# The last four passes of a pipelined transformer kernel, written out call by call on all five engines

## What is computed

```
x = x + tanh(g_xattn[0]) * L0_xattn(layernorm(x), ctx, ctx)   # q, k, v with relu; relu(q k') v, no softmax
x = x + tanh(g_ffn[0])   * L0_ffn(layernorm(x))               # 512 -> 1024 -> 1024 -> 256, weights +1 or -1
x = x + tanh(g_xattn[1]) * L1_xattn(layernorm(x), ctx)        # best key of each token, then softmax over 77 keys, 16 heads
x = x + tanh(g_ffn[1])   * L1_ffn(layernorm(x))               # shared expert + top 8 of 64 experts, 128 rows each

# L1_ffn:
probs = softmax(x @ gate_w); w, idx = top_k(probs, 8)
pos = running count of the tokens that chose an expert        # over all tokens, in order
buf[e, slot] = x[tok]; act = silu(gate) * up; out_e = act @ expert_down_w
y = sum over the 8 chosen of out_e[e, slot] * w, where pos < 128
```

## Time and profile before

| | us |
|---|---|
| median of 3 runs | 1708.06 |
| lowest and highest | 1705.67, 1710.39 |
| the profiled execution | 1710.62 |
| its span in the trace | 1708.9 |
| busy in the span: PE, DVE, ACT, POOL | 1533.9, 1312.4, 1018.1, 1006.8 |

### The profile page before, as it was taken

One profiled execution on the slowest core, in us unless ns is written; L12 is line 12 of the kernel. 1 busy time (PEld: TensorE's weight loads), 2 busy tenths in 40 slices (PEclk: granted clock), 3 DMA queues, 4 the chain that ended last, 5 costly groups with the idle time before them and its releaser, 6 DMA issues.

```text
span 1708.9 us, 50224 instructions
## 1 busy us (share of the span) xinstructions
PE 1533.9 (90%) x15780; PEld 1308.4 (77%) x15780; DVE 1312.4 (77%) x4611; ACT 1018.1 (60%) x2789; POOL 1006.8 (59%) x1517
## 2 busy tenths in 40 slices
PE   2879999999999999999999999999999986478885
PEld 1768888888888888888888888888888865367774
DVE  5468888888888888888888888888888865456564
ACT  2456666666666666666666666666666653334443
POOL 3114566666666666666666666666666644365554
PEclk8989999999999999999999999999999997799998
DMA  7624444444433333433333333333333334558886
GB/s 224 190 55 101 101 102 100 93 98 99 87 74 79 84 82 83 92 77 77 80 84 80 84 77 77 77 80 81 80 81 77 91 67 111 126 139 207 201 196 129
DMA packets 382151, 176.21 MB, mean 103 GB/s; under 512 B 310175, under 2 KB 371561, under 8 KB 382104
## 3 DMA queue, kind: packets, MB, share of 16 engines
q1 hardware_dynamic: 348312, 156.45, 38.8%
q0 software_dynamic: 33792, 19.17, 6.6%
HBM read 51.63 MB, written 111.84 MB: 96 GB/s over the span
## 4 chain that ended last, share of the span: by engine, by line
PE 62%; DMA 14%; issue 8%; DVE 7%; ACT 4%; POOL 3%; SPq 1%; POOLq 0%; DVEq 0%; ACTq 0%
PE bank L1306 24%; PE bank L1200 9%; DMA out<-h_h,aid 9%; PE ps_yo L1200 7%; PE ps_yo L1322 3%; PE bank L1288 3%; DMA pt<-p_hl 3%; PE ps_m L1200 2%; PE ps_pt L1200 2%; PE ps_lg L1370 2%; PE ps_pt L1272 2%; ACT p L977 2%; POOL table L722 2%; PE ps_pt L1265 1%; PE ps_tr L1200 1%
## 5 line engine op out<-in xcount | busy, mean ns | idle before, releaser
L722 POOL DMA_INDIRECT table<-xs,slot x496 | 511.7, 1032 | 189.5 <-issue 158.3
L769 POOL TENSOR_TENSOR rs<-nt,minushalf 128x2 f32<-128x2 f32 x128 | 95.6, 747 | 311.4 <-DVE nt L1756 310.9
L977 ACT ACTIVATE p<-ps_lg,rmax 128x77 f32<-128x77 f32 x1024 | 248.6, 335 | 50.9 <-DVE rmax L1868 49.4
L1306 PE MATMUL bank<-h_h,held 128*128 128x256 f16 x2048 | 266.2, 273 | 1.4 <-DVE h_l L1798 1.1
L1306 PE MATMUL bank<-h_l,held 128*128 128x256 f16 x2048 | 265.7, 273 | 0.0
L1306 PEld LDWEIGHTS bank<-h_l,held 128*128 128x128 f16 x2048 | 200.6, 98 | 23.4
L1306 PEld LDWEIGHTS bank<-h_h,held 128*128 128x128 f16 x2048 | 195.4, 98 | 27.6 <-issue 1.6
L1798 DVE SCALAR_TENSOR_TENSOR h_l<-bank,h_h 128x512 f16<-128x512 f32 x256 | 172.7, 684 | 33.3 <-ACT h_h L954 23.8
L949 ACT ACTIVATE h_h<-bank 128x512 f16<-128x512 f32 x128 | 76.4, 597 | 156.1 <-PE bank L1288 156.1
L1200 PE MATMUL bank<-xt,gu_h 128*128 128x256 f16 x1024 | 157.1, 277 | 3.1 <-DVE ac L1964 2.9
L1288 PE MATMUL bank<-xt,held 128*128 128x256 f16 x1024 | 134.1, 282 | 22.8 <-DMA xt<-rows_hl 13.4
(11 more groups left out here) (271 smaller groups left out, 3884.8 us busy)
## 6 DMA issues: line engine op xcount, KB each, us to landing
ew<-in_e_wts SPq DMA_DIRECT2D x48, 384.0 KB, 3.9
table<-xg SPq DMA_DIRECT2D x8, 1284.0 KB, 14.8
xg<-table SPq DMA_DIRECT2D x64, 160.5 KB, 3.4
xs<-xr SPq DMA_DIRECT2D x31, 320.0 KB, 2.8
x<-in_x SPq DMA_DIRECT2D x32, 256.0 KB, 2.8
out<-x SPq DMA_DIRECT2D x32, 256.0 KB
table<-xs,slot POOLq DMA_INDIRECT x496
held<-in_e_wts SPq DMA_DIRECT2D x16, 384.0 KB, 5.0
```

Of the source, the lines that this page charges most:

```text
L722: return g.indirect_dma_start(out=table, out_offset=bass.IndirectOffsetOnAxis(ap=slots[:, t, k:k + 1], axis=0), in_=rows[:, t, :], in_offs ...
L769: g.tensor_tensor(rs[i][:, :], nt[i][:, 0, :], minushalf[:, :], ALU.pow).then_inc(ln_root[i], 1)
L977: ins = a.activation(p32[r % 2][:, h * S2:(h + 1) * S2], ps_lg[:, g_, h % HB * S2:(h % HB + 1) * S2], ACT.Exp, bias=rmax[r % 2][:, h:h + 1])
L1306: ins = mm(two(bank[j % 2])[:, m % 2, :], wb1[:, k, m * P:(m + 1) * P], hp[:, k, :], start=(i == 0 and k == 0), stop=(i == 1 and k == FK - 1))
```

## The change

The calls of `body` behind the loop are replaced, on every engine, by the calls that they would make, each with its block as a constant, in another order. The functions themselves, the loop, the prologue and the expert phase are the same. No wait is added or removed; where a wait stands in the engine's order changes. SP's list is short and stands here in full; of the others a few lines.

```diff
@@ sync
             body(NB - 2)
             for i in range(4):
                 load_held(i)
-            body(NB - 1)
+            turn_p(2, NB - 3)
+            turn_p(3, NB - 3)
+            turn(1, NB - 1)
+            pass_rows(NB - 4)
+            stack(NB - 2)
+            turn(3, NB - 3)
+            turn_p(0, NB - 2)
+            turn_p(1, NB - 2)
+            store_x4(NB - 4)
+            turn_p(2, NB - 2)
+            turn_p(3, NB - 2)
+            pass_rows(NB - 3)
+            stack(NB - 1)
+            turn(3, NB - 2)
+            turn_p(0, NB - 1)
+            store_x4(NB - 3)
+            turn_p(1, NB - 1)
+            turn_p(2, NB - 1)
+            pass_rows(NB - 2)
+            turn_p(3, NB - 1)
             for i in range(4, 8):
                 load_held(i)
             for e in range(XD - 1):
                 load_weights(e, e)
-            body(NB)
+            turn(3, NB - 1)
             sp.wait_ge(l2_rdy, NB)
             for i in range(8, 12):
                 load_held(i)
-            body(NB + 1)
+            pass_rows(NB - 1)
+            store_x4(NB - 2)
             for i in range(12, 16):
                 load_held(i)
-            body(NB + 2)
+            store_x4(NB - 1)
@@ gpsimd
-            body(NB - 1)
-            body(NB)
-            body(NB + 1)
-            body(NB + 2)
+            keep_x2(NB - 3)
+            ln_coef(1, NB - 1)
+            ln_coef(2, NB - 2)
+            keep_x1(NB - 1)
+            scatter('a', NB - 4)
...
@@ tensor
-            body(NB - 1)
-            body(NB)
-            body(NB + 1)
+            d_gu(0, NB - 4)
+            c_lg(2, NB - 3)
...
             d_gu(0, NB - 1)
             d_gu(1, NB - 1)
+            d_cp(NB - 1)
             d_gu(2, NB - 1)
-            d_cp(NB - 1)
...
@@ vector, the last block's part D
             d_max(NB - 1)
+            d_choose(NB - 1)
             d_gu(0, NB - 1)
-            d_choose(NB - 1)
...
```

More of the change, by code:

```diff
@@ new lines, in _ @@
+            c_qp(NB - 2)
+            ln_norm(3, NB - 3, x3, xr)
+            high(3, NB - 3, xr[:, :, 0:D])
+            c_stack(NB - 2)
+            b_l1(0, NB - 1)
+            b_l1(1, NB - 1)
+            c_vb(NB - 2)
+            c_exp(0, NB - 2)
+            d_gu(0, NB - 3)
+            c_exp(1, NB - 2)
+            d_ac(0, NB - 3)
+            d_gu(1, NB - 3)
+            c_phi(0, NB - 2)
+            d_gu(2, NB - 3)
+            c_exp(2, NB - 2)
+            d_ac(1, NB - 3)
+            c_exp(3, NB - 2)
@@ new lines, in _ @@
+            c_qp(NB - 1)
+            ln_norm(3, NB - 2, x3, xr)
+            high(3, NB - 2, xr[:, :, 0:D])
+            c_stack(NB - 1)
+            c_vb(NB - 1)
+            c_exp(0, NB - 1)
+            c_exp(1, NB - 1)
+            c_phi(0, NB - 1)
+            c_exp(2, NB - 1)
+            d_gu(0, NB - 2)
+            c_exp(3, NB - 1)
+            d_gu(1, NB - 2)
+            d_ac(0, NB - 2)
+            c_phi(1, NB - 1)
+            c_exp(4, NB - 1)
+            d_gu(2, NB - 2)
+            c_exp(5, NB - 1)
@@ new lines, in _ @@
+            c_phi(2, NB - 1)
+            d_ac(1, NB - 2)
+            d_route(NB - 2)
+            c_exp(6, NB - 1)
+            c_exp(7, NB - 1)
+            d_ac(2, NB - 2)
+            c_phi(3, NB - 1)
+            d_gu(3, NB - 2)
+            d_ac(3, NB - 2)
+            high(4, NB - 1, att[:, :, :])
+            ln_norm(3, NB - 1, x3, xr)
+            high(3, NB - 1, xr[:, :, 0:D])
+            d_route(NB - 1)
+            d_gu(0, NB - 1)
+            d_gu(1, NB - 1)
+            d_ac(0, NB - 1)
@@ L1155, in rows_copy @@
+            d_ac(1, NB - 1)
+            d_gu(2, NB - 1)
+            d_gu(3, NB - 1)
+            d_ac(2, NB - 1)
+            d_ac(3, NB - 1)
             def rows_copy(e, u):
@@ new lines, in _ @@
+            c_lg(7, NB - 3)
+            b_l1(5, NB - 2)
+            b_l1(6, NB - 2)
+            d_dn(0, NB - 4)
+            d_dn(1, NB - 4)
+            c_av(1, NB - 3)
+            b_l1(7, NB - 2)
+            d_cp(NB - 4)
+            c_av(2, NB - 3)
+            b_l2(0, NB - 2)
+            b_l2(1, NB - 2)
+            c_av(3, NB - 3)
+            b_l0(0, NB - 1)
+            across(4, NB - 3)
+            b_l0(1, NB - 1)
+            c_wc(NB - 3)
+            across(2, NB - 2)
+            b_l0(2, NB - 1)
@@ new lines, in _ @@
+            c_lg(4, NB - 2)
+            b_l1(4, NB - 1)
+            c_lg(5, NB - 2)
+            b_l1(5, NB - 1)
+            b_l1(6, NB - 1)
+            c_lg(6, NB - 2)
+            c_av(0, NB - 2)
+            d_cp(NB - 3)
+            c_lg(7, NB - 2)
+            d_dn(0, NB - 3)
+            d_dn(1, NB - 3)
+            c_av(1, NB - 2)
+            b_l1(7, NB - 1)
+            c_av(2, NB - 2)
+            b_l2(0, NB - 1)
+            b_l2(1, NB - 1)
+            c_av(3, NB - 2)
+            across(4, NB - 2)
@@ L1598, in _ @@
+            c_av(0, NB - 1)
+            c_lg(7, NB - 1)
+            c_av(1, NB - 1)
+            d_cp(NB - 2)
+            c_av(2, NB - 1)
+            d_dn(0, NB - 2)
+            c_av(3, NB - 1)
+            across(4, NB - 1)
+            d_dn(1, NB - 2)
+            c_wc(NB - 1)
             d_route(NB - 1)
@@ new lines, in _ @@
+            c_max(7, NB - 3)
+            c_plo(2, NB - 3)
+            d_ac(2, NB - 4)
+            d_ac(3, NB - 4)
+            c_norm(0, NB - 3)
+            c_plo(3, NB - 3)
+            ln_shift(1, NB - 1)
+            b_l1(2, NB - 2)
+            c_norm(1, NB - 3)
+            d_x4(NB - 4)
+            low(1, NB - 1, xn[1][:, :, :])
+            d_pos(NB - 4)
+            b_l1(3, NB - 2)
+            c_norm(2, NB - 3)
+            d_slots(NB - 4)
+            b_x2(NB - 2)
+            c_norm(3, NB - 3)
@@ new lines, in _ @@
+            d_gu(3, NB - 3)
+            c_plo(1, NB - 2)
+            c_max(5, NB - 2)
+            d_choose(NB - 3)
+            d_ac(2, NB - 3)
+            d_ac(3, NB - 3)
+            c_plo(2, NB - 2)
+            c_max(6, NB - 2)
+            d_pos(NB - 3)
+            b_l1(2, NB - 1)
+            c_norm(0, NB - 2)
+            c_max(7, NB - 2)
+            d_x4(NB - 3)
+            c_norm(1, NB - 2)
+            c_plo(3, NB - 2)
+            b_l1(3, NB - 1)
+            d_slots(NB - 3)
+            c_norm(2, NB - 2)
@@ new lines, in _ @@
+            b_x2(NB - 1)
+            ln_sums(2, NB - 1, x2, x2_ok)
+            c_norm(3, NB - 2)
+            ln_moments(2, NB - 1)
+            ln_shift(2, NB - 1)
+            low(4, NB - 2, att[:, :, :])
+            low(2, NB - 1, xn[2][:, :, :])
+            c_x3(NB - 2)
+            ln_sums(3, NB - 2, x3, x3_ok)
+            ln_moments(3, NB - 2)
+            c_qp(NB - 1)
+            ln_shift(3, NB - 2)
+            c_argmax(NB - 1)
+            c_counts(NB - 1)
+            low(3, NB - 2, xr[:, :, 0:D])
@@ L2148, in _ @@
+            d_choose(NB - 2)
+            c_norm(0, NB - 1)
+            d_ac(1, NB - 2)
+            c_plo(3, NB - 1)
+            d_pos(NB - 2)
+            c_norm(1, NB - 1)
+            d_gu(3, NB - 2)
+            d_ac(2, NB - 2)
+            c_norm(2, NB - 1)
+            d_ac(3, NB - 2)
+            d_slots(NB - 2)
+            c_norm(3, NB - 1)
+            low(4, NB - 1, att[:, :, :])
+            d_x4(NB - 2)
+            c_x3(NB - 1)
+            ln_sums(3, NB - 1, x3, x3_ok)
             ln_moments(3, NB - 1)
```

243 lines of the change are left out of this document (233 added, 10 removed).

## The result

| | before | changed kernel |
|---|---|---|
| median, us (4 runs each, side by side) | 1707.11 | 1687.58 |
| lowest and highest | 1705.67, 1710.39 | 1683.97, 1689.96 |
| the profiled execution (the one before is not among its four runs) | 1710.62 | 1689.96 |
| its span | 1708.9 | 1688.2 |

The ratio is 0.9881, with a 95% interval of 0.9854 to 0.9908: 19.5 us less by the medians, where the forecast had 17.8 less.

The account below looks back on a forecast made before the run. The tail was taken as a chain of block 31 alone, held by what stands in its way. Seven stage terms sum to -17.8 us: 1692.8 for the profiled execution, 1690.3 against the 1708.06 median; range 1683 to 1701.

Parts of the forecast that it names:

- Pass 31: Pass from 1348.6 on, 48.0 us: PE's 4.51 us wait for `att` goes, clock nearly 1.00; 43.0 us, minus 5.0.
- End of the first feed-forward: Block 31's stage after pass 31, 24.8 us: short PE waits shrink; 21.4 to 26, taken as 23.5, minus 1.3.
- To the first logits: Block 31's next stage, 22.2 us: DVE's 4.34 us wait goes, with most of PE's 5.46; minus 5.4.
- Softmax: Block 31, first logits to last `c_av`, 28.4 us: transpose saves 3.2, logits order 1.88 and 1.8; 21.5, minus 6.9.
- To part D's input: Block 31, last `c_av` to part D input's landing, 15.9 us: DVE order and seven loads cost 0.5 each; plus 1.0.
- My 13.3 us: Price of seven weight loads and the copy behind them, ahead of part D's transpose, wanted 15.9 us later: 2.6 in hand.
- Part D: Block 31, part D up to the first expert, 19.2 us: earlier choice, slots and `x4`; minus 1.2.
- Expert phase: Last window, 201.8 us: part of the last four weight loads still under way at the first `xg`; plus 1.0.
- the weights land in front: Rival: weight loads ahead of block 31's part D transpose make part D start late; 1698.3 us, chance 0.13.
- The waits only change places: Rival: stages two and four don't gain, as one more engine waits for PE's order; 1698.5 us, chance 0.12.
- The clock comes back: Rival: fuller stages three to five are granted 2.4 GHz on PE; another -3.8 us, 1686.5, chance 0.12.
- POOL's queue: Rival: weight loads slow POOL's 29 scatters, so first expert's rows come late; over 5.1 us slower; 0.04 with other losses.

Follow-up runs that it names:

- the second profile: The changed kernel called again with nothing edited, beside its variants: median 1685.06 us, ratio 0.9861 to the kernel before, span 1682.1 us.
- the kernel with eleven loads: The changed kernel with four more weight loads, eleven instead of seven, ahead of the transpose of block 31's part D input: ratio 0.9875 to the kernel before.

## Why the prediction was right, and where not

The time was right: 1690.3 forecast, 1687.6 measured, and the range held it. By its steps (the first profile and the second):

- **Pass 31**, 43.0 forecast: 46.1 and 42.7. The mechanism is shown from both sides: with the `pow` in front of the scatters 42.3 to 46.4 us, with POOL's old list 48.3 to 56.1. I had priced the transposes behind four loads at up to 1 us on PE; it is 2.03 in one execution (1.1 in the second), and the clock takes 1.7 more (16 matmuls at a pitch of 0.21 us instead of 0.11).
- **End of the first feed-forward**, 23.5 forecast: 22.2 and 22.0. Right in sign, the gain was sized too small: 1.3 against 2.6. PE is busy for 21.31 us of it, so it came to within 1 us of my lower end of 21.4. I had read the edits here as small repairs. The experiments show more: with POOL's list alone, the computing engines' alone, or these two, this stage is 29.7 to 32.3 us, through `d_slots(29)` and through `pt`, in one case by way of SP's own wait for scatters. I had seen neither of these two couplings.
- **To the first logits**, 16.8 forecast: 17.8 and 16.6. The wait of 4.34 us on DVE fell to 0.85. Shown by undoing it: with POOL's old list the stage takes 23.3 us, and DVE waits again, 5.96 us; with POOL's and SP's new lists alone it takes 17.9.

```profile
1435.16 0.16 DVE L1971 TENSOR_TENSOR nb<-nt,rs 128x2 f32<-128x2 f32 x1 [5.96 <-POOL rs L789]
```

  The computing engines' lists alone have 16.7 us here with POOL's old list. That is no counterexample: PE's wait of 6.72 us comes first, so POOL is through its scatters in time (its `pow` waits 2.18 us for DVE), and this stage and the one before it last 46.5 us together, against 47.0 before and 40.1 in the changed kernel.
- **Softmax**, 21.5 forecast: 20.0 and 20.2. The transpose's part was 3.2 us; from the end of the low half to the last `c_av` it is 3.9 us now and was 6.8:

```profile
1448.11 0.83 DVE L2141 TENSOR_TENSOR p_hl<-p,p_hl 128x640 f16<-128x640 f32 x1 [0.17 <-ACT p_hl L1062]
```

```profile
1447.24 0.69 SPq L485 DMA_DIRECT2D xs<-xr  x1
1449.00 1.37 SPq L474 DMA_TRANSPOSE pt<-p_hl  x1
1450.42 2.11 SPq L575 DMA_DIRECT2D held<-in_e_wts  x4
1452.57 1.73 SPq L572 DMA_DIRECT2D ew<-in_e_wts  x3
...
1463.61 1.25 SPq L463 DMA_TRANSPOSE xt<-rows_hl  x1
...
1472.57 2.21 SPq L575 DMA_DIRECT2D held<-in_e_wts  x4
```

  The other two parts had 3.7 us, and took 5.5: from the first logits to the end of the last low half it is 16.1 us (1448.94 - 1432.85) and was 21.6. ACT's wait of 1.88 us before its last exponentials is gone. So the estimate of 1.8 us from PE's idle time was the weak term: by difference it wants about 3.6, and no run takes it apart. That `pass_rows(30)` costs nothing held: it went out at 1447.24, 14.4 us after the first logits (15 forecast), and the transpose found SP free at 1449.00.
- **To part D's input**, plus 1.0 forecast: -1.5 and -0.1. This is the step that failed. The seven loads were issued at 1450.42 and the transpose at 1463.61, when its rows were ready; it landed 3.64 us later, as one without loads in front. The DMA row of 1448 to 1500, 1.3 us to a number, shows the queue empty by 1461:

```profile
GB/s 231 136 219 227 333 310 331 392 388 117 0 0 8 191 254 367 324 271 61 296 228 265 237 390 208 0 0 0 163 277 29 120 42 85 24 120 232 171 310 196
```

  So the seven took under 11 us with block 30's scatters beside them. My 13.3 us were read from the first load's issue to the first scatter behind the copy. That holds the copy too, which is no small transfer as I called it (320 KB, a load has 384), and two transposes had been queued ahead of the loads and two more behind the copy. A time from issue to landing holds everything that was in the queue.
- **Part D**, 18.0 forecast: 19.8 and 17.3. It can't be judged to the 1.2 us of the forecast, since the clock (0.76 and 0.89) moves it by more. That the scatters would wait for their slots and not for POOL was right:

```profile
1477.93 0.97 POOL L742 DMA_INDIRECT table<-xs_z,slot_z  x1 [3.07 <-DVE slot_z L2219]
```

- **Expert phase**, 202.8 forecast: 201.1 and 200.1. The plus 1.0 for leftover weights isn't there, for the same reason: the DMA row above is at zero again from 1480.5 to 1484.4, so the last four loads, issued at 1472.57, were through before the first `xg` went out at 1484.65.

So four of the seven stages came out 1.1 to 2.7 us shorter than forecast, and in the first profile pass 31 and part D gave 4.9 us of that back. Its stages sum to -18.9 us against the earlier trace rows, those of the second profile to -25.6: the forecast of -17.8 lies near the medians' -19.5, and 6.0 us from the -23.8 of the second set. Its terms were too cautious, so part of the match with the first set is luck.

Of the rivals, *the weights land in front* is excluded by the row above and by the profile of the kernel with eleven loads. *The waits only change places* did not come for the whole, but it is just what single lists do. *The clock comes back* is not seen: PE's clock in stages three to five is 0.69, 0.68, 0.85 and 0.84, 0.75, 0.61, against 0.71, 0.74, 0.61 before. The softmax, with PE busy for 64 to 68% of it instead of 55%, is still in good part at 1.2 GHz. The Trainium skill (TensorE: Matmul & The Clock Gate, What's actually happening) says that activity releases the clock. By that rule this case was to come; here PE's busy share rose and the granted clock of the softmax went from 0.74 to 0.68 and 0.75. *POOL's queue* is out, by POOL's waits between 1347 and 1487, to set beside the earlier trace rows:

```profile
POOL rs L789 <- DVE nt L2024: 29.6, 5, 16.4
POOL table L742 <- issue: 21.0, 62, 3.1
```

Its scatters' issue waits are as before, 0.34 us in the mean (20.5 us in 59 waits before), and it has idle time to give.

## What to carry to other kernels

Where each engine takes its instructions in a fixed order, an order is one decision over all engines: a list tried on one engine alone can come out slower, as SP's did here by 5.3 us, though the whole is 20 us faster. So look for a short operation with a waiting engine behind it (here a `pow` of 0.7 us) that stands behind work that itself waits, move it in front, and ask of every reordered engine which tile, transpose, copy or scatter another engine still delivers in the old order. Price a queue of DMAs by when the transfer rate falls to zero, not by when something behind it starts.

## What the runs showed that I had not expected

- Bulk loads clear fast: seven of 384 KB in under 11 us beside scatters, eleven in at most 15.6 us, at up to 392 GB/s in a slice of 1.3 us, while the copy of 320 KB issued right behind such loads had taken 8.0 and 9.3 us until its scatter. The case that speaks for the queue's order is the kernel with the computing engines' lists alone: a transpose issued right behind seven loads and a copy took 8.32 us, and without such loads in the queue 3.5 to 3.9. The rule of the Trainium skill that a ring is taken in order (DMA: Bandwidth & Descriptors, Queues, rings and completion order) agrees with that; only my price was wrong.
- A wait can look like the queue and be the issuing engine. All lists but SP's left PE waiting 7.62 us for a transpose behind seven loads, and 4.9 us of it was SP standing at a wait for scatters.
- One wait of 2.03 us of PE was followed by some 3.4 us at 1.2 GHz in an otherwise full stage, which made it cost 3.7 us in all.
- Two executions of the same kernel differ by 6 us in the span and by 3.4 us in a stage. A profile's stage can be compared with another's to no better than that unless both are taken more than once.
